# Routing and scattering the last batch earlier in a fused attention and mixture-of-experts kernel

## The chip, the cores and the metric

The kernel runs on one core of one Trainium2 chip. The metric is the device time of one launch in microseconds (us). Engines are named as the profile names them: PE is TensorE (PEld its weight loads), DVE VectorE, ACT ScalarE, POOL GpSimd, and SP the queue that issues most of the direct transfers.

## The reference, cut to what matters

Four batches of 1024 tokens with 128 channels go through one attention layer without learned projections, and then through a layer of eight experts, of which each token takes two. All is float32.

```
x = x + attention(layernorm(x))                  # scores = (x*w_lhs) @ (x*w_rhs).T, softmax, @ x
xf = layernorm(x)                                # 4096 tokens, 128 channels
logits = xf @ router_w.T                         # 8 experts
topk_probs, topk_idx = top_k(softmax(logits), 2) # renormalised to a sum of 1
h = gelu_new(xf @ w_fc[e] + b_fc[e])             # hidden size 512
out = h @ w_proj[e] + b_proj[e]
x = x + sum over the token's two experts of out * gate
```

## The kernel before, in words

**Attention.** The loop over `b` takes one batch of 1024 tokens at a time, as eight token tiles of 128 in two halves. While PE scores batch b, the engines finish batch b-1: the residual (`add_attention`), the second layernorm (`take_stats2`, `take_moments2` on DVE, `scale_ln2` on POOL, `make_h2` and `high_h2` on ACT, `split_h2` on DVE), and the routing.

**Routing a batch** is a chain over four engines. `picks` (DVE, 13 steps) finds the two experts of each token; `find_gap` (DVE) gives the gap of the two logits, and waits for the layernorm scale of the batch's last half from `scale_ln2` on POOL; `gate_powers` (POOL) makes the gate of it; `rank_round` (PE) counts the earlier tokens of each expert; `keep_ranks` and `find_slots` (DVE) make each token's slot numbers and end in the semaphore `meta_made`. Then `dispatch(b, i)` on POOL scatters one tile of rows from `stage` to `slots` in device memory: 16 scatters for a batch (8 token tiles, 2 experts each).

**Experts.** When attention ends, `slots` holds the tokens sorted by expert, and 47 expert tiles are worked through: 24 of 256 rows, then 23 of 128 rows mixed with the last eight large ones. `ORDER` is the sequence. Each engine has a hand-written `step(k)`:

- SP `load(k)` reads the tile from `slots`, once its start is known. Tiles 0 to 7 need table 1 and batches 0 and 1 scattered, tiles 8 to 15 table 2 and batch 2, and tile 16 table 3 and batch 3.
- PE step k: `turn_slots(k+2)` (transposes, L1285), `up(k)` (L1298 to L1300), `down(k-2)` (L1319). So the transposes of tile 8 stand at the start of step 6 and those of tile 16 at the start of step 14.
- ACT step k: `copy_xT(k+2)`, `gelu(k)`, and in the first steps the layernorm of batch 3.
- DVE step k: pieces of the next table (`make_table`), `keep_rows(k)`, then `add_bias(k-3)` and `gate(k-3)`. `down(k)` on PE waits for `add_bias(k-2)`.
- POOL step k: `give_back(k-4)`, a scatter of 128 results for each half tile, once `up(k)` is done.

**The last batch** has no attention behind it that could hide its routing, so its routing is laid between the first expert tiles, at steps that are written out by hand. Its ranks lie in one half of a PSUM bank of `av_ps` that `down` of odd tiles also writes, so one `down` has to wait for `ranks_kept`, which is what `keep_ranks` signals. In the kernel before, PE counts the ranks at the end of step 4 and `down(3)` in step 5 waits for `ranks_kept`; DVE finds the slots in step 5; POOL scatters the batch in its steps 6 and 7:

```
LAST_SCATTERS = {6: range(0, 8), 7: range(8, SCATTERS)}
```

The tables are made by DVE alone: table 2 in steps 0 to 4 (`second_table`), table 3 in 6 to 9 (`late_table`), table 4 in 10 to 13 (`small_table`).

Of the kernel before, what the change touches and what calls it, by code (L numbers as in the profile page):

```python
# [23 lines left out]
def preln_attention_moe(nc, x, w_lhs, w_rhs, router_wT, w_fc, b_fc, w_proj, b_proj, out):  # L24
# [60 lines left out]
    with ExitStack() as ctx:  # L85
# [138 lines left out]
        place = sb("place", [P, H], F32)  # L224
        small_place = sb("small_place", [P, 1], F32)
# [454 lines left out]
        def _(pool):  # L680
# [104 lines left out]

            def gate_powers(r):

                mine = within(r)
                pool.wait_ge(gap_made, r + 1)
                if r >= 1:  # L790
                    pool.wait_ge(slots_made, 4 * r)
                pool.tensor_tensor(gate2[:, mine], euler[:, mine], gap[:, mine], ALU.pow).then_inc(gate_exp, 1)
# [80 lines left out]
            for i in range(11, 15):  # L873
                dispatch(B - 2, i)
            gate_powers(len(ROUNDS) - 1)
            for i in range(15, SCATTERS):
                dispatch(B - 2, i)


            LAST_SCATTERS = {6: range(0, 8), 7: range(8, SCATTERS)}  # L880
# [21 lines left out]
        def _(act):  # L902
# [132 lines left out]
            def step(k, a):  # L1035
                if tile_there(k + 2):
                    copy_xT(k + 2, (a + 2) % NB)
                if tile_there(k):
                    gelu(k, a)

                if k < 2:
                    make_h2(2 * B - 2, 2 + k)
                    if k == 1:
                        high_h2(2 * B - 2)
                if 2 <= k < 6:
                    make_h2(2 * B - 1, k - 2)
                    if k == 5:
                        high_h2(2 * B - 1)
# [9 lines left out]
        def _(pe):  # L1058
# [244 lines left out]
            def down(k, a):  # L1303
# [6 lines left out]
                if k == 3:  # L1310
                    pe.wait_ge(ranks_kept, len(ROUNDS))
# [11 lines left out]
            def step(k, a):  # L1323
# [6 lines left out]
                if k == 4:  # L1330

                    pe.wait_ge(biased_made, 2)
                    rank_round(len(ROUNDS) - 1)
# [18 lines left out]
        def _(dve):  # L1352
# [394 lines left out]
            choose = picks(last)  # L1747

# [38 lines left out]
            def step(k, a):  # L1787

                if k == 0:
                    take_stats2(2 * B - 1)  # L1790
                    take_moments2(2 * B - 1)
                if 1 <= k < 4:
                    steps(choose, (5, 5, 3)[k - 1])
                if k == 3:
                    find_gap(last)
                    split_h2(2 * B - 2)
                if k < 5:
                    steps(second_table, (3, 4, 4, 2, 20)[k])
                if k == 5:
                    keep_ranks(last)  # L1800
                    find_slots(last)
                if k == 7:
                    split_h2(2 * B - 1)
# [57 lines left out]
```

## Time and profile before

| | |
|---|---|
| median of 3 runs | 310.88 us (310.45 to 312.26) |
| span of the profiled execution | 352.5 us |
| time of the profiled execution outside its span | none is shown |
| mean granted clock of TensorE | 0.928 |
| busy in the span | PE 281.2, DVE 230.5, ACT 197.3, POOL 178.5 us |
| scatters to `slots` (POOL) | 64 |
| scatters to `results` (POOL) | 71 |

The profile is of one execution, and its span is 41.6 us longer than the median of the plain runs. A line of a timeline gives the start in us from the span's start, the duration, the engine, the source line, the operation, the output and inputs by the program's names, and in brackets how long the engine had been idle and what ended that. "issue" is idle time in which the profile shows nothing that the engine waited for.

### The profile page before, as it was taken

The page shows a single profiled execution, that of the slowest core. Times are in us where ns is not written, and L with a number is a line of the kernel's source. Part 1 is how long each engine was busy: PE and PEld are TensorE (multiplying, and loading weights), DVE is VectorE, ACT ScalarE, POOL GpSimd, SP SyncE. Part 2 cuts the span into 40 slices and gives each one's busy share as a digit, 9 for nine tenths or more (in the row PEclk, how much of TensorE's full clock was granted, in tenths as well). Part 3 has the DMA queues.
Part 4 walks back from the last instruction along what each step waited for, and adds up shares of the span by engine and source line. Part 5 has one row for each costly group of instructions (what it writes and reads, how often), then busy time and mean ns, then how long its engine had stood idle before and what let it go on. Part 6 is the DMA issues. An engine that isn't in the chain of part 4 may idle for free.

```text
span 352.5 us, 8201 instructions
## 1 busy us (share of the span) xinstructions
PE 281.2 (80%) x2223; PEld 247.1 (70%) x2223; DVE 230.5 (65%) x972; ACT 197.3 (56%) x427; POOL 178.5 (51%) x243
## 2 busy tenths in 40 slices
PE   7999999999949987799496353999969999978200
PEld 3689997989748975689486233999959989977200
DVE  4898988889636896887775224685545555634265
ACT  3363778873648634365694213577658888855100
POOL 8030260285757358585777575455554555444500
PEclk9999999999979999999999685899999999989855
DMA  6930000012110001014213221113222222210199
GB/s 214 420 145 0 3 0 3 0 38 87 55 40 32 2 23 48 31 48 126 68 48 108 70 71 53 47 40 94 74 73 80 70 62 79 65 37 32 37 376 338
DMA packets 15450, 28.51 MB, mean 81 GB/s; under 512 B 3904, under 2 KB 9920, under 8 KB 15152
## 3 DMA queue, kind: packets, MB, share of 16 engines
q1 hardware_dynamic: 10800, 17.93, 15.4%
q0 software_dynamic: 4608, 10.07, 8.6%
q8 instruction: 20, 0.33, 0.4%
q14 instruction: 22, 0.18, 0.2%
HBM read 15.83 MB, written 12.16 MB: 79 GB/s over the span
## 4 chain that ended last, share of the span: by engine, by line
PE 65%; DVE 12%; issue 10%; another core or an unknown queue 4%; ACT 3%; POOL 2%; DMA 2%; POOLq 0%; ACTq 0%; DVEq 0%; SPq 0%
PE av_ps L1319 19%; PE av_ps L1114 14%; PE sc_ps L1300 5%; PE sc_ps L1298 5%; PE sc_ps L1299 4%; DVE neg_piece L1435 4%; PE bank L1285 3%; PE sc_ps L1103 2%; DVE res L1823 2%; PE bank L1090 1%; PE bank L1099 1%; DVE res L1821 1%; PE bank L1092 1%; PE bank L1091 1%
## 5 line engine op out<-in xcount | busy, mean ns | idle before, releaser
L887 POOL DMA_INDIRECT results<-prob,result_row x71 | 68.2, 961 | 62.3 <-PE sc_ps L1300 26.6
L1319 PE MATMUL av_ps<-raw_proj,raw_fc 128*128 x568 | 78.1, 287 | 19.1 <-issue 16.0
L1319 PEld LDWEIGHTS av_ps<-raw_proj,raw_fc 128*128 128x128 f32 x568 | 70.9, 199 | 22.1 <-issue 21.7
L1031 ACT ACTIVATE raw_fc<-sc_ps,bfc,scale_down 128x256 f32<-128x256 f32 (+1 forms) x188 | 80.7, 516 | 3.7 <-remote 3.5
L783 POOL DMA_INDIRECT slots<-stage,slot x64 | 62.6, 978 | 30.4 <-issue 20.2
L1114 PE MATMUL av_ps<-h_all,prob 128*128 128x137 f32 x512 | 74.3, 288 | 0.1
L1114 PEld LDWEIGHTS av_ps<-h_all,prob 128*128 128x128 f32 x512 | 67.7, 192 | 4.2 <-DVE res L1463 1.4
L1777 DVE TENSOR_TENSOR h_all<-av_ps,bpr 128x256 f32<-128x256 f32 (+1 forms) x47 | 16.9, 360 | 63.5 <-remote 35.0
L1023 ACT ACTIVATE h_all<-bank 128x512 f16<-128x512 f16 (+1 forms) x47 | 23.0, 493 | 58.9 <-remote 36.1
L1298 PE MATMUL sc_ps<-h_all,wfc_hi 128*128 128x256 f16 (+1 forms) x188 | 44.2, 252 | 4.2 <-issue 2.9
L1300 PE MATMUL sc_ps<-h_all,wfc_lo 128*128 128x256 f16 (+1 forms) x188 | 44.1, 252 | 2.8 <-issue 2.8
L1299 PE MATMUL sc_ps<-h_all,wfc_hi 128*128 128x256 f16 (+1 forms) x188 | 44.3, 252 | 0.5 <-issue 0.5
L1435 DVE TENSOR_REDUCE neg_piece<-bank 128x1 f32<-128x512 f32 x32 | 22.0, 688 | 14.3 <-remote 6.4
L936 ACT ACTIVATE prob<-sc_ps 128x512 f32<-128x512 f32 x32 | 18.1, 599 | 11.5 <-PE sc_ps L1103 10.3
L1435 DVE TENSOR_REDUCE neg_piece<-sc_ps 128x1 f32<-128x512 f32 x32 | 21.9, 685 | 2.6 <-remote 1.4
L1298 PEld LDWEIGHTS sc_ps<-h_all,wfc_hi 128*128 x188 | 18.8, 100 | 6.8 <-issue 5.1
L926 ACT ACTIVATE again<-bank 128x512 f32<-128x512 f32 x16 | 9.6, 597 | 22.0 <-DVE neg_piece L1435 21.7
L1784 DVE TENSOR_SCALAR prob<-h_all,row_gate 128x128 f32<-128x128 f32 x71 | 20.0, 352 | 1.8 <-DVE h_all L1777 0.2
L1299 PEld LDWEIGHTS sc_ps<-h_all,wfc_hi 128*128 x188 | 18.8, 100 | 3.0 <-issue 2.0
L1300 PEld LDWEIGHTS sc_ps<-h_all,wfc_lo 128*128 x188 | 18.7, 100 | 2.6 <-issue 1.2
L1285 PE MATMUL bank<-ident,slots_in 128*128 128x128 f16 x142 | 16.1, 224 | 4.9 <-issue 4.9
L1090 PE MATMUL bank<-hT_hi,q_hi 128*128 128x512 f32 x32 | 14.6, 457 | 3.7 <-DVE next_slot L1570 2.1
(184 smaller groups left out, 516.7 us busy)
## 6 DMA issues: line engine op xcount, KB each, us to landing
slots_in<-slots SPq DMA_DIRECT2D x24, 132.0 KB
raw_fc<-in_w_fc_dram SPq DMA_DIRECT2D x1, 2048.0 KB, 11.3
raw_proj<-in_w_proj_dram SPq DMA_DIRECT2D x1, 2048.0 KB, 15.7
raw_fc<-results SPq DMA_DIRECT2D x4, 512.0 KB, 5.1
raw_proj<-results SPq DMA_DIRECT2D x4, 512.0 KB, 8.0
out_dram<-res SPq DMA_DIRECT2D x8, 256.0 KB, 6.1
res<-in_x_dram SPq DMA_DIRECT2D x3, 512.0 KB, 5.9
slots_in<-slots SPq DMA_DIRECT2D x23, 66.0 KB
```

The source lines that it names most:

```text
L783: pool.indirect_dma_start(out=slots[:, :], out_offset=bass.IndirectOffsetOnAxis(ap=slot[:, n, k:k + 1], axis=0), in_=stage[:, b % 2, t, :] ...
L887: pool.indirect_dma_start(out=results[:, :], out_offset=bass.IndirectOffsetOnAxis(ap=result_row[a][:, h:h + 1], axis=0), in_=gated[a][h], ...
L1023: act.activation(xT[:, a % NH, 0:n], bank[a % 2][:, :].bitcast(F16)[:, 0:n], ACT.Copy).then_inc(xT_made, 1)
L1031: ins = act.activation(hid[:, a % NH, c, 0:halves_of(k) * P], up_ps(k, c), ACT.Gelu_apprx_tanh, bias=bfc[:, e, c:c + 1], scale=scale_down[ ...
L1114: mm = pe.matmul(att[:, t, 0:AUG], probT[:, m % RING, t * P:(t + 1) * P], h_aug[:, b % 2, exp_rows(n), :], start=(n % BT == 0 and t % 2 == ...
L1285: mm = pe.transpose(o[:, part * w + h * P:part * w + (h + 1) * P], x, ident16[:, :])
L1298: pe.matmul(o, wfc_hi[:, e, of], xT[:, a % NH, 0:w], start=True, stop=False, skip_group_check=True)
L1299: pe.matmul(o, wfc_hi[:, e, of], xT[:, a % NH, w:2 * w], start=False, stop=False, skip_group_check=True)
L1300: mm = pe.matmul(o, wfc_lo[:, e, of], xT[:, a % NH, 0:w], start=False, stop=True, skip_group_check=True)
L1319: mm = pe.matmul(o, hid[:, a % NH, c, rows], wpr[:, e, c, :], start=(c == 0 and h == 0), stop=(c == HC - 1), skip_group_check=True)
L1435: dve.tensor_reduce(neg_piece[:, r // TU, r % TU, c:c + 1], block_bank(n), AX_X, ALU.max, negate=True).then_inc(max_made, 1)
L1784: ins = dve.tensor_scalar(gated[k % NR][h], biased[:, a % NH, h, :], row_gate[:, a, h:h + 1], None, ALU.mult)
```

## The change

Six edits in one. (1) On POOL a memset of one column of a new scratch tile `apart` follows each of the 64 scatters to `slots`; nothing reads it. (2) On POOL `gate_powers` of the last batch stands ahead of the last five scatters of batch 2, not ahead of the last one. (3) The scatters of batch 3 stand in POOL's steps 4 and 6, not 6 and 7. (4) On ACT the layernorm of batch 3 is done in steps 0, 2 and 3, not 0 to 5. (5) On PE the ranks are counted at the end of step 2, not 4, and `down(1)` waits for `ranks_kept`, not `down(3)`. (6) On DVE the statistics, the picks and the gap of the last batch stand ahead of step 0; `keep_ranks` moves from step 5 to 3, `find_slots` from 5 to 4, the two `split_h2` from 3 and 7 to 2 and 5.

```diff
             def dispatch(b, i):
...
                                         in_=stage[:, b % 2, t, :], in_offset=None).then_inc(dispatched[b % 2], 16)
 
+                pool.memset(apart[:, b * K * BT + i:b * K * BT + i + 1], 0.0)
...
             scale_ln2(2 * B - 1)
-            for i in range(11, 15):
+            gate_powers(len(ROUNDS) - 1)
+            for i in range(11, SCATTERS):
                 dispatch(B - 2, i)
-            gate_powers(len(ROUNDS) - 1)
-            for i in range(15, SCATTERS):
-                dispatch(B - 2, i)
...
-            LAST_SCATTERS = {6: range(0, 8), 7: range(8, SCATTERS)}
+            LAST_SCATTERS = {4: range(0, 8), 6: range(8, SCATTERS)}
...
-                if k < 2:
-                    make_h2(2 * B - 2, 2 + k)
-                    if k == 1:
-                        high_h2(2 * B - 2)
-                if 2 <= k < 6:
-                    make_h2(2 * B - 1, k - 2)
-                    if k == 5:
+                if k == 0:
+                    make_h2(2 * B - 2, 2)
+                    make_h2(2 * B - 2, 3)
+                    high_h2(2 * B - 2)
+                if 2 <= k < 4:
+                    make_h2(2 * B - 1, 2 * k - 4)
+                    make_h2(2 * B - 1, 2 * k - 3)
+                    if k == 3:
                         high_h2(2 * B - 1)
...
-                if k == 3:
+                if k == 1:
                     pe.wait_ge(ranks_kept, len(ROUNDS))
...
-                if k == 4:
-
-                    pe.wait_ge(biased_made, 2)
+                if k == 2:
+
                     rank_round(len(ROUNDS) - 1)
...
             choose = picks(last)
+            take_stats2(2 * B - 1)
+            take_moments2(2 * B - 1)
+            steps(choose, 13)
+            find_gap(last)
...
-                if k == 0:
-                    take_stats2(2 * B - 1)
-                    take_moments2(2 * B - 1)
-                if 1 <= k < 4:
-                    steps(choose, (5, 5, 3)[k - 1])
+                if k == 2:
+                    split_h2(2 * B - 2)
                 if k == 3:
-                    find_gap(last)
-                    split_h2(2 * B - 2)
+                    keep_ranks(last)
+                if k == 4:
+                    find_slots(last)
                 if k < 5:
                     steps(second_table, (3, 4, 4, 2, 20)[k])
                 if k == 5:
-                    keep_ranks(last)
-                    find_slots(last)
-                if k == 7:
                     split_h2(2 * B - 1)
```

**DVE, where step 0 begins.** Before, behind the variance of the batch's last half, three steps of table 2 and then `keep_rows(0)`, which waits for tile 0:

```order
L1491 TENSOR_SCALAR var<-moments 128x4 [waits ln2_rstd,ln2_moments]
L485 TENSOR_TENSOR per_expert<-per_expert,ends 128x8 [waits dve_chain]
L488 TENSOR_TENSOR past<-tile_id,per_expert 128x64 [waits dve_chain]
L492 TENSOR_SCALAR capped<-per_expert 128x16 [waits dve_chain]
L1762 SCALAR_TENSOR_TENSOR gate_parts<-slots_in,of_expert 128x2 [waits xs_in0]
L1764 SCALAR_TENSOR_TENSOR gate_parts<-slots_in,of_expert 128x2
L1766 SCALAR_TENSOR_TENSOR chosen_row<-slots_in,of_expert 128x2
L1769 TENSOR_TENSOR row_gate<-gate_parts 128x2 [waits row_parts]
```

Of the change, from the end of the picks (`taken`) to the same place, with the step that waits for `ln2_rstd` (POOL's scale) and the load of the expert numbers ahead of them:

```order
L1542 TENSOR_TENSOR pick<-pick,first_id 128x64 [waits route_chain]
L1550 TENSOR_TENSOR taken<-pick 128x2x32 [waits route_chain]
L1556 TENSOR_TENSOR step_down<-best 128x8
L1561 TENSOR_TENSOR gap<-step_down,rstd 128x8 [waits gate_exp,ln2_rstd,route_chain]
L587 TENSOR_LOAD turn_experts
L587 ISA x2
L487 TENSOR_TENSOR per_expert<-per_expert,ends 128x8 [waits dve_chain]
L490 TENSOR_TENSOR past<-tile_id,per_expert 128x64 [waits dve_chain]
L494 TENSOR_SCALAR capped<-per_expert 128x16 [waits dve_chain]
L1768 SCALAR_TENSOR_TENSOR gate_parts<-slots_in,of_expert 128x2 [waits xs_in0]
L1770 SCALAR_TENSOR_TENSOR gate_parts<-slots_in,of_expert 128x2
```

All 13 picks, the gap and its wait now stand ahead of the table and of tile 0's rows.

**PE, the ranks.** Before, the count (L1136, L1142) stands behind `down(2)` and ahead of the transposes of tile 7 (`xs_in7`):

```order
L1319 MATMUL av_ps<-raw_proj,raw_fc 128x128 x5
L1136 MATMUL av_ps<-taken,before 128x80 [waits taken_made,biased_made]
L1142 MATMUL av_ps<-taken,ones 128x72
L1142 MATMUL av_ps<-taken,ones 128x64
L1142 MATMUL av_ps<-taken,ones 128x56
L1142 MATMUL av_ps<-taken,ones 128x48
L1142 MATMUL av_ps<-taken,ones 128x32
L1142 MATMUL av_ps<-taken,ones 128x24
L1142 MATMUL av_ps<-taken,ones 128x16
L1142 MATMUL av_ps<-taken,ones 128x8
L1285 MATMUL bank<-ident,slots_in 128x128 [waits xT_made,xs_in7]
L1285 MATMUL bank<-ident,slots_in 128x128 x3
```

Of the change it stands behind `down(0)`, ahead of the transposes of tile 5 (the line numbers are three higher), and no longer waits for `biased_made`:

```order
L1322 MATMUL av_ps<-raw_proj,raw_fc 128x128 x5
L1139 MATMUL av_ps<-taken,before 128x80 [waits taken_made]
L1145 MATMUL av_ps<-taken,ones 128x72
L1145 MATMUL av_ps<-taken,ones 128x64
L1145 MATMUL av_ps<-taken,ones 128x56
L1145 MATMUL av_ps<-taken,ones 128x48
L1145 MATMUL av_ps<-taken,ones 128x32
L1145 MATMUL av_ps<-taken,ones 128x24
L1145 MATMUL av_ps<-taken,ones 128x16
L1145 MATMUL av_ps<-taken,ones 128x8
L1288 MATMUL bank<-ident,slots_in 128x128 [waits xT_made,xs_in5]
L1288 MATMUL bank<-ident,slots_in 128x128 x3
```

The count has moved two tiles forward, past two `up` and two `down`.

**POOL, behind the scale of the last half.** Before, four scatters to `slots`, the gate, one scatter, and then the results of tiles 0 and 1:

```order
L748 TENSOR_TENSOR shift<-neg_mean,rstd 128x4 [waits ln2_mean,ln2_rstd]
L783 DMA slots<-stage,slot 32768x132 [waits meta_made,h2lo_made] x4
L792 TENSOR_TENSOR gate<-euler,gap 128x8 [waits slots_made,gap_made]
L783 DMA slots<-stage,slot 32768x132 [waits meta_made,h2lo_made]
L887 DMA results<-prob,result_row 22528x128 [waits gated_made,row_made,stepped]
L887 DMA results<-prob,result_row 22528x128
L887 DMA results<-prob,result_row 22528x128 [waits gated_made,row_made,stepped]
L887 DMA results<-prob,result_row 22528x128
```

Of the change the gate stands first; each scatter has a memset behind it:

```order
L750 TENSOR_TENSOR shift<-neg_mean,rstd 128x4 [waits ln2_mean,ln2_rstd]
L796 TENSOR_TENSOR gate<-euler,gap 128x8 [waits slots_made,gap_made]
L785 DMA slots<-stage,slot 32768x132 [waits meta_made,h2lo_made]
L788 MEMSET apart 128x1
L785 DMA slots<-stage,slot 32768x132 [waits meta_made,h2lo_made]
L788 MEMSET apart 128x1
L785 DMA slots<-stage,slot 32768x132 [waits meta_made,h2lo_made]
L788 MEMSET apart 128x1
```

The eight first scatters of the last batch (not shown) follow directly on the 16th of batch 2, ahead of the results of tile 0, where before the results of tiles 0 and 1 stood ahead of them.

## Rows read from the trace of the kernel before

**Rows 1.** The page: span, busy time of each engine, shares of the chain.

```profile
span 352.5 us, 8201 instructions
...
PE 281.2 (80%) x2223; PEld 247.1 (70%) x2223; DVE 230.5 (65%) x972; ACT 197.3 (56%) x427; POOL 178.5 (51%) x243
...
PE 65%; DVE 12%; issue 10%; another core or an unknown queue 4%; ACT 3%; POOL 2%; DMA 2%; POOLq 0%; ACTq 0%; DVEq 0%; SPq 0%
```

**Rows 2.** Windows: busy us of each engine, TensorE clock, in one stretch.

```profile
core 0: us, PE busy (x) PEld busy (x) DVE busy (x) ACT busy (x) POOL busy (x), PEclk, DMA share, GB/s
...
192.00:195.00 3.00, 0.27 (x1) 0.37 (x2) 0.00 (x0) 0.00 (x0) 2.26 (x3) 1.00 0.31 99
```

**Rows 3.** Timeline of PE: start, us, instruction, at three tiles, and its end.

```profile
187.74 0.39 PE L1285 MATMUL bank<-ident,slots_in 128*128 128x128 f16 x4
...
225.46 0.39 PE L1285 MATMUL bank<-ident,slots_in 128*128 128x128 f16 x4
...
238.74 0.39 PE L1285 MATMUL bank<-ident,slots_in 128*128 128x128 f16 x4
...
327.55 1.15 PE L1319 MATMUL av_ps<-raw_proj,raw_fc 128*128 x8 [0.24 <-ACT raw_fc L1031]
```

**Rows 4.** Windows over a fall of the clock.

```profile
97.10:100.50 3.40, 1.37 (x10) 1.08 (x8) 0.00 (x0) 0.00 (x0) 2.54 (x3) 1.00 0.15 51
100.50:107.30 6.80, 4.21 (x14) 3.73 (x15) 3.38 (x15) 5.09 (x11) 3.45 (x5) 0.50 0.07 22
```

**Rows 5.** Timeline of DVE: last batch and the tiles' own work.

```profile
168.00 0.87 DVE L1478 BATCH_NORM_STATS2 stats<-res 128x6 f32<-128x128 f32 x4 [0.75 <-issue]
...
173.23 0.16 DVE L496 TENSOR_TENSOR per_expert<-per_expert,used 128x8 f32<-128x8 f32 x1
...
174.19 0.21 DVE L1762 SCALAR_TENSOR_TENSOR gate_parts<-slots_in,of_expert 128x2 f32<-128x2 f32 x1
...
174.85 0.22 DVE L1544 SCALAR_TENSOR_TENSOR lg<-pick,lg 128x64 f32<-128x64 f32 x1
...
178.20 0.68 DVE L1498 TENSOR_TENSOR stage<-h,stage 128x512 f16<-128x512 f32 x1
```

**Rows 6.** Timeline of DVE: ranks and slots of the last batch.

```profile
185.24 0.23 DVE L1567 TENSOR_TENSOR rank<-av_ps,next_slot 128x64 f32<-128x64 f32 x1 [1.32 <-PE av_ps L1142]
...
185.58 0.35 DVE L1577 TENSOR_TENSOR pick<-pick,rank 128x64 f32<-128x64 f32 x2
...
187.45 0.22 DVE L1762 SCALAR_TENSOR_TENSOR gate_parts<-slots_in,of_expert 128x2 f32<-128x2 f32 x1
```

**Rows 7.** Timeline of POOL: scatters before the last batch.

```profile
172.10 1.05 POOL L745 TENSOR_TENSOR rstd<-var,minus_half 128x4 f32<-128x4 f32 x1
...
177.88 0.95 POOL L783 DMA_INDIRECT slots<-stage,slot  x1 [0.30 <-issue]
178.86 1.67 POOL L792 TENSOR_TENSOR gate<-euler,gap 128x8 f32<-128x8 f32 x1
180.73 1.03 POOL L783 DMA_INDIRECT slots<-stage,slot  x1 [0.20 <-issue]
182.06 0.96 POOL L887 DMA_INDIRECT results<-prob,result_row  x1 [0.30 <-issue]
...
185.80 0.95 POOL L887 DMA_INDIRECT results<-prob,result_row  x1 [1.52 <-PE sc_ps L1300]
```

**Rows 8.** Groups of POOL: the scatter and a memset of one column.

```profile
L783 POOL DMA_INDIRECT slots<-stage,slot x64 | 62.6, 978 | 30.4 <-issue 20.2 <-DVE stage L1595 7.3 <-ACT prob L936 2.8
...
L701 POOL MEMSET digit<- 128x1 f32 x8 | 0.3, 99 | 0.0
```

**Rows 9.** Timeline of SP: the issue of tile 8's load.

```profile
185.04 0.00 SPq L662 DMA_DIRECT2D slots_in<-slots  x1
```

**Rows 10.** Timeline of PE: the projection of tile 1.

```profile
177.52 1.95 PE L1319 MATMUL av_ps<-raw_proj,raw_fc 128*128 x16
```

**Rows 11.** Timeline of ACT: its start of tile 1.

```profile
173.33 0.60 ACT L1023 ACTIVATE h_all<-bank 128x512 f16<-128x512 f16 x1 [3.26 <-remote]
```

More of the change, by code:

```diff
@@ L224, in preln_attention_moe @@
         place = sb("place", [P, H], F32)
+        apart = sb("apart", [P, K * NT], F32)
         small_place = sb("small_place", [P, 1], F32)
```

## The prediction

> **What bounds the kernel now.** I read the page first: the chain that ended last lies 65% on PE, 12% on DVE and 10%, some 35 us, on "issue", time in which nothing that the profile shows was waited for [rows 1]. So PE sets the end, and a tenth of the span has no cause in the program. A window of 3 us at 192 shows what such time looks like: PE is busy 0.27 us, DVE and ACT not at all, while POOL goes on scattering [rows 2]; one at 97 to 100 us is of the kind too [rows 4]. The timeline of PE gives its size. From the transposes of tile 12 (step 10, 225.46) to those of tile 16 (step 14, 238.74) a step lasts 3.32 us; from tile 8's (step 6, 187.74) to tile 12's four steps last 37.72 us, 24.4 more than 4 x 3.32 [rows 3]. With this and the smaller ones of its kind (about 4 us at 98 to 102, 2 us of half clock behind it [rows 4], 3 us of ACT at 170 to 173 [rows 11], and by the same windows some 9 us elsewhere) I come to about 42 us. The span is 352.5 us [rows 1] and no time outside it is shown; the plain runs take 310.88. So I hold that the plain runs don't have these stretches (352.5 - 42 = 310.5), take them out, and give what is left in the clock of the profile, around the edit. The sum below is a difference of two such reckonings, added to 310.88.
>
> **The place that counts.** Two loads on SP are held by scatters: tile 8's by batch 2, tile 16's by batch 3. If PE comes to step 14 before tile 16 is there, the last batch's scatters bound the kernel; if it comes later, PE's own steps do. I need four times: when PE comes to step 14 and when tile 16 lies in SBUF, each before and after.
>
> **Before, tile 16.** POOL ends batch 2's last scatter at 181.76 and does the results of tile 0 at 182.06. Those of tile 1 begin at 185.80, 1.52 us late, since they wait for `up(5)` [rows 7]; without the 1.4 us that DVE's and PE's gaps cost here, about 184.5. From there POOL isn't idle: 2 results, 8 scatters, 2 results, 8 scatters, 20 in all, each 0.96 us and 0.30 us of issue [rows 7, 8], 1.26 us: the last ends at 184.5 + 25.2 = 209.7. From the end of batch 2's last scatter to the issue of tile 8's load lie 185.04 - 181.76 = 3.3 us [rows 7, 9]. From issue to transposes 187.74 - 185.04 = 2.7 us is the upper bound [rows 3, 9]; PE came there straight from `down(3)`, so I take 1.2. Tile 16 can be turned at 209.7 + 3.3 + 1.2 = 214.2 (213.6 to 216, with 2.7 and POOL's start at 185.8 for the upper end). **Before, PE.** Step 6 begins at 187.74 [rows 3], or about 1.2 us earlier without the gaps: 186.5. Eight steps of 3.32 are 26.6: step 14 at 213.1. So the scatters decide, by about 1 us: 214.2.
>
> **After, the new wait.** PE counts the ranks behind `down(0)`, but `down(1)` waits for `ranks_kept`, and DVE keeps the ranks only in step 3. What DVE has ahead of that: (a) `find_gap` waits for POOL's scale, ready at 172.10 + 1.05 = 173.15 [rows 7]; that lies behind six scatters whose memsets add 0.2, so the gap is made by 173.4. The 11 picks and `taken`, ahead of it, are 0.26 us each and fit between 168.7 and 172.2. (b) Loading the expert numbers, 0.75 (the idle time ahead of the statistics, at the same place of the program) [rows 5]. (c) `keep_rows` three times, 174.85 - 174.19 = 0.66, say 0.7: 2.1 [rows 5]. (d) Table 2: four steps are 174.19 - 173.23 = 0.96, eleven 2.3 [rows 5]. (e) `split_h2` 0.6 (its 0.68 overlaps the next) [rows 5]. (f) The ranks 185.58 - 185.24 = 0.34 [rows 6]. Sum: 173.4 + 0.75 + 2.1 + 2.3 + 0.6 + 0.34 = 179.5. In the profile before, `down(1)` began at 177.52 [rows 10], and that was late: `up(3)` waited for ACT, which had lost 3.26 us [rows 11]; without it about 175.3. PE stands still from 175.3 to 179.5, 4.2 us. Queued behind it are `turn_slots(6)`, `up(4)` and all after; ACT has `gelu(2)` behind it and waits with PE.
>
> From 179.5 PE has `down(1)` (1.8) and steps 4 and 5 (2 x 3.32): step 6 at 188.0. Nothing on DVE holds it longer: `add_bias(0)` ends at 181.0, then the slots (187.45 - 185.58 = 1.87 [rows 6]), the rest of table 2 (7 steps, 1.3), `keep_rows(4)` and `add_bias(1)` come to 185.8, and `down(3)` starts at 186.2. Table 2 is ready at 184.6, batch 2's last scatter ends at 182.1 with the memsets, so tile 8's load is out by 185.7 and doesn't hold PE either. ACT's layernorm of two token tiles a step costs it 0.5 us more in steps 0, 2 and 3, and is covered by PE's wait; without the wait it would delay `gelu(3)` by under 1 us, which PE needs two steps later. Step 14 follows at 188.0 + 26.6 = 214.6.
>
> **The clock.** In 97.1 to 100.5 PE was busy 1.37 of 3.4 us, and in the next 6.8 us its granted clock was 0.50, that is 1.2 GHz [rows 4]. A stand of 4.2 us is of that kind. PE's work from 179.5 on would then run at half speed for 2 to 4 us and lose 1 to 2 us. The trace can't say that it falls; I put it at 60%. Step 14 is at 214.6 without and 215.6 to 216.6 with it.
>
> **After, tile 16.** `meta_made` comes with the slots, at 183.3. POOL waits for it from 182.1: here the earlier place of the scatters buys an idle engine. Then 8 scatters, 4 results, 8 scatters. **The memset** measures 0.10 us [rows 8]. Between two scatters lie 0.30 us; around the gate they are 0.03 and 0.20 [rows 7], so a memset between should make it 0.03 + 0.10 + 0.20 = 0.33, 0.03 more; at most it adds its whole 0.10. I take 0.03 (the gate is the nearest row) and 1.29 a scatter: 183.5 + 16 x 1.29 + 4 x 1.26 = 209.2, with 0.10 a memset 210.3. Tile 16 can be turned at 209.2 + 3.3 + 1.2 = 213.7 (to 216.3). For the other 48 memsets, 1.4 to 4.8 us of POOL, the cover is POOL's waits for DVE and ACT between the batches (10.1 us ahead of scatters alone, 7.3 + 2.8 [rows 8]). One rule speaks against the price: the Trainium skill (SBUF — State Buffer, section "SBUF: two separate sides") says that GpSimd and a VectorE operation of certain kinds lock each other out of a shared port for a whole instruction. By it each of the 16 could wait for a DVE operation, 0.2 to 0.7 us, and tile 16 would come up to 11 us later. The scatters of this trace don't show it: they take 0.95 and 0.96 us beside a busy DVE and 0.96 in the mean [rows 7, 8].
>
> **The sum.** Before, tile 16 is turned at 214.2 (scatters). After, it is 214.6 without a fall of the clock and about 216.1 with it (PE). The difference is +0.4 or +1.9, weighed +1.3; so 312.2 us. Behind step 14 nothing changes: PE ended 90 us later (327.55 + 1.15 - 238.74 [rows 3]), 83 without some 7 us of empty stretches, at 297; POOL's 65 remaining results, 82 us from 209.7 on, are done at 292.
>
> **The rivals.** (A) *The wait at `down(1)` costs nothing*, since tile 16 comes later than I reckon in both kernels (the upper ends, 216 before). Then the time is the difference of the two scatter chains, 213.7 - 214.2 = -0.5, or 0 with dearer memsets: 310.4 to 311. For it: no trace shows tile 16 late, since in the profile PE was later than all scatters. (B) *Faster*: PE's stand is shorter than 1 us because DVE gets to the ranks by 176, and what goes is the wait for the ranks in step 5 and for tile 16: at most 214.2 - 213.1 = 1.1 us, with 1.3 for a later start of POOL 2.4 us: 308.5 to 309.3. It decides if DVE's 6.1 us between gap and ranks are 3 or less. Or the empty stretches aren't gone in the plain runs and the memsets, which set the scatters apart, shorten them: 305 to 309. For it, they all lie where scatters follow one another; against it, the 42 us. (C) *Worse*: POOL's scale comes later, or the clock falls twice, or the memsets meet the port: 314 to 317.
>
> **How the numbers follow.** The forecast case (PE bound, +0.2 to +3) gets 0.52, A 0.20, B 0.15, C 0.13. The measurement tells apart about 0.5%, 1.55 us. Of the forecast case about half lies above +1.55; with C, slower gets 0.39. B gives faster 0.15; A and the other half are 0.46. The range goes from inside B to inside C: 309.3 to 315.3.
>
> **What would show it.** In the profile after: PE idle ahead of the first matmul of `down(1)`, released by DVE's `next_slot`, 3 to 5 us; the clock at 0.50 behind it; `find_gap` on DVE released by POOL's `rstd`; POOL idle about 1.3 us ahead of the first scatter of batch 3; a memset of 0.10 us and scatters 1.29 us apart. I am wrong if `down(1)` starts without a wait, if tile 16's transposes wait for SP in the kernel after, or if the span falls to near the plain time, which would say that the memsets act on the empty stretches.
>
> The Trainium skill (Runtime: NRT & Kernel Launch, section "The ~15µs preamble/postamble breakdown") says that a profile's total lies some 6 us above the plain time whatever the kernel; here it is 41.6, so by that rule 35 us would be real, the end would hang on the empty stretches, and case B's second half would gain weight. That no number above rests on.

## The result, and the profile after

| | kernel before | changed kernel |
|---|---|---|
| median of plain runs | 310.81 us (310.2 to 312.52, 12 runs) | 312.82 us (311.84 to 314.54, 12 runs) |
| ratio to before | | 1.0067, 95% interval 1.0049 to 1.0085 |
| profiled execution, span | 352.5 us [rows 1] | 311.0 us, own time 312.78 us |

The change costs 2.0 us, 0.7%. 312.2 was predicted, in a range of 309.3 to 315.3. The page of the changed kernel, its span, engine and chain lines:

```profile
span 311.0 us, 8265 instructions
...
PE 269.4 (87%) x2223; PEld 241.8 (78%) x2223; DVE 230.1 (74%) x972; ACT 196.7 (63%) x427; POOL 185.5 (60%) x307
...
PE 60%; POOL 12%; issue 10%; DVE 8%; DMA 4%; ACT 3%; SPq 1%; POOLq 1%; DVEq 0%; ACTq 0%
```

The span is 41.5 us shorter than that of [rows 1], though the kernel got slower. The empty stretches of [rows 2] are gone. So no time of this page may be set against one of [rows 1 to 11] without a common mark. I use `rstd` on POOL, the scale that the gap needs: it starts at 172.10 before [rows 7] and at 164.04 here, so 8.06 us less. The timeline of PE, from the projection of tile 1 to the transposes of tiles 6, 8 and 16:

```profile
171.78 3.78 PE L1322 MATMUL av_ps<-raw_proj,raw_fc 128*128 x16 [6.30 <-DVE next_slot L1572]
175.35 0.63 PE L1288 MATMUL bank<-ident,slots_in 128*128 128x128 f16 x4
...
182.60 0.39 PE L1288 MATMUL bank<-ident,slots_in 128*128 128x128 f16 x4
...
209.16 0.39 PE L1288 MATMUL bank<-ident,slots_in 128*128 128x128 f16 x4
```

PE stands still for 6.30 us, for the ranks, as forecast. The 16 matmuls of `down(1)` then take 3.78 us instead of the 1.95 of [rows 10]. Tile 16 is there when PE wants it: its row has no idle time. The timeline of DVE shows why the ranks are late:

```profile
165.18 0.20 DVE L1561 TENSOR_TENSOR gap<-step_down,rstd 128x8 f32<-128x8 f32 x1 [1.86 <-issue]
166.12 0.17 DVE L487 TENSOR_TENSOR per_expert<-per_expert,ends 128x8 f32<-128x8 f32 x1 [0.74 <-issue]
...
171.38 0.16 DVE L1572 TENSOR_TENSOR next_slot<-next_slot,av_ps 128x8 f32<-128x8 f32 x1
...
172.48 0.42 DVE L1783 TENSOR_TENSOR h_all<-av_ps,bpr 128x256 f32<-128x256 f32 x1
```

DVE is idle for 1.86 us ahead of `find_gap`. The row calls it "issue", but POOL's `rstd` below ends at 165.09, 0.09 us before the gap starts, and the gap waits for it. Then the expert numbers are loaded (the 0.74 us of idle time in the second row), and steps 0 to 2 follow. The last row is `add_bias(0)`. The windows (stretches of 5 us, columns as in [rows 2]) show the clock:

```profile
165.00:170.00 5.00, 0.48 (x5) 0.19 (x2) 3.81 (x21) 1.05 (x3) 4.27 (x8) 0.98 0.04 14
170.00:175.00 5.00, 3.22 (x15) 3.23 (x16) 4.59 (x29) 4.38 (x10) 3.16 (x6) 0.50 0.16 54
175.00:180.00 5.00, 5.00 (x44) 4.56 (x44) 3.81 (x22) 2.30 (x5) 3.47 (x7) 0.84 0.27 64
```

PE's granted clock is 0.50 (1.2 GHz) behind the stand. POOL's timeline, the scale and the gate, the end of batch 2, the start and the end of batch 3:

```profile
164.04 1.05 POOL L747 TENSOR_TENSOR rstd<-var,minus_half 128x4 f32<-128x4 f32 x1
...
165.46 1.64 POOL L796 TENSOR_TENSOR gate<-euler,gap 128x8 f32<-128x8 f32 x1
...
173.42 0.12 POOL L788 MEMSET apart<- 128x1 f32 x1
175.96 0.96 POOL L785 DMA_INDIRECT slots<-stage,slot  x1 [2.41 <-DVE stage L1597]
176.91 0.11 POOL L788 MEMSET apart<- 128x1 f32 x1
177.22 0.96 POOL L785 DMA_INDIRECT slots<-stage,slot  x1 [0.19 <-issue]
...
199.96 0.95 POOL L785 DMA_INDIRECT slots<-stage,slot  x1 [0.19 <-issue]
```

Scatters start 1.26 us apart, which is also what 0.96 us and 0.30 us of idle time make without a memset [rows 7, 8]. The memset lies in what had been 0.30 us of idle time, of which 0.19 are left.

### The profile page after: what moved, and what is told of

It is laid out like the page before. It is cut to its first block, busy times and chain, and to the rows that moved or that the text cites. A ratio compares the mean times of both kernels' runs of the same rounds, so it can differ in the third digit from the quotient of the medians.

```text
span 311.0 us, 8265 instructions
## 1 busy us (share of the span) xinstructions
PE 269.4 (87%) x2223; PEld 241.8 (78%) x2223; DVE 230.1 (74%) x972; ACT 196.7 (63%) x427; POOL 185.5 (60%) x307
## 4 chain that ended last, share of the span: by engine, by line
PE 60%; POOL 12%; issue 10%; DVE 8%; DMA 4%; ACT 3%; SPq 1%; POOLq 1%; DVEq 0%; ACTq 0%
PE av_ps L1322 21%; PE av_ps L1117 10%; POOL slots L785 8%; PE sc_ps L1301 5%; PE sc_ps L1302 4%; PE sc_ps L1303 4%; DVE neg_piece L1437 4%; DMA raw_proj<-results 3%; PE bank L1288 2%; PE bank L1093 1%; PE sc_ps L1106 1%; PE bank L1095 1%; PE bank L1094 1%; POOL apart L788 1%; SPq L675 1%
## 5 line engine op out<-in xcount | busy, mean ns | idle before, releaser
L1322 PE MATMUL av_ps<-raw_proj,raw_fc 128*128 x568 | 74.2, 282 | 6.4 <-DVE next_slot L1572 6.3
L1322 PEld LDWEIGHTS av_ps<-raw_proj,raw_fc 128*128 128x128 f32 x568 | 68.7, 196 | 7.4 <-issue 7.0
L1117 PE MATMUL av_ps<-h_all,prob 128*128 128x137 f32 x512 | 73.2, 285 | 0.7 <-DVE lg_part L1468 0.6
L1117 PEld LDWEIGHTS av_ps<-h_all,prob 128*128 128x128 f32 x512 | 66.8, 190 | 4.6 <-DVE res L1465 1.7
L1301 PE MATMUL sc_ps<-h_all,wfc_hi 128*128 128x256 f16 (+1 forms) x188 | 43.0, 248 | 1.1 <-ACT raw_fc L1033 1.1
L1302 PE MATMUL sc_ps<-h_all,wfc_hi 128*128 128x256 f16 (+1 forms) x188 | 42.9, 247 | 0.0
L1303 PE MATMUL sc_ps<-h_all,wfc_lo 128*128 128x256 f16 (+1 forms) x188 | 42.9, 247 | 0.0
L948 ACT ACTIVATE h<-res,shift,rstd 128x128 f32<-128x128 f32 x32 | 14.2, 486 | 6.9 <-DVE stage L1500 4.0
```

What stands on the lines that cost most here:

```text
L1117: mm = pe.matmul(att[:, t, 0:AUG], probT[:, m % RING, t * P:(t + 1) * P], h_aug[:, b % 2, exp_rows(n), :], start=(n % BT == 0 and t % 2 == ...
L1301: pe.matmul(o, wfc_hi[:, e, of], xT[:, a % NH, 0:w], start=True, stop=False, skip_group_check=True)
L1302: pe.matmul(o, wfc_hi[:, e, of], xT[:, a % NH, w:2 * w], start=False, stop=False, skip_group_check=True)
L1303: mm = pe.matmul(o, wfc_lo[:, e, of], xT[:, a % NH, 0:w], start=False, stop=True, skip_group_check=True)
L1322: mm = pe.matmul(o, hid[:, a % NH, c, rows], wpr[:, e, c, :], start=(c == 0 and h == 0), stop=(c == HC - 1), skip_group_check=True)
```

## The experiments

The kernel before was timed in each group of runs: 310.41, 310.38 and 310.37 us. Ratios are to these; a ratio can differ from the quotient of two medians by 0.1%. The theories of an expectation are numbered in it.

**1. The memsets alone, on the kernel before.**

```diff
                 pool.indirect_dma_start(out=slots[:, :], ...).then_inc(dispatched[b % 2], 16)
+                pool.memset(apart[:, b * K * BT + i:b * K * BT + i + 1], 0.0)
```

> The kernel before with one thing of the change alone: GpSimd clears a column of the scratch tile behind each scatter to the slots. Theory 1 (the memsets lie in time in which GpSimd would be idle between two scatters anyway, and nobody's work waits for them): time as of before, 310.8 us within 0.5%; and since the empty stretches of before's profile (rows 2, about 42 us) are a distortion of the profiled execution, they go with the memset alone: span about 309 instead of 352.5, and its rows then show for the first time how the plain run of before goes. Theory 2 (each memset delays the next scatter by its 0.1 us, 128 times, and the queue behind POOL ends later): 1 us or more slower. Theory 3 (the empty stretches are also in plain runs, in part): faster by more than 1 us.

Measured: 310.59 us, ratio 1.0013 (0.9996 to 1.0031); span 310.7 us. The time is that of theory 1, and theories 2 and 3 fall. The empty stretches are gone too, as theory 1 said; whether the memsets took them away, only experiment 2 can tell.

**2. The changed kernel without the memsets.**

```diff
-                pool.memset(apart[:, b * K * BT + i:b * K * BT + i + 1], 0.0)
```

> The changed kernel without the memsets. Theory 1 (the memset acts on the profile alone): time as of the changed kernel, 312.8 us (+0.6% to before), but the profiled span back at about 350 us with empty stretches where GpSimd scatters back to back. Theory 2 (the memsets are what the 2 us went to): back at 310.8 us. Theory 3 (the memsets hid a part of the loss): 314 us or more.

Measured: 312.75 us, ratio 1.0084 (1.0061 to 1.0108), as the changed kernel; span 309.8 us. The timeline of POOL there:

```profile
198.70 0.96 POOL L784 DMA_INDIRECT slots<-stage,slot  x1 [0.30 <-issue]
199.96 1.01 POOL L784 DMA_INDIRECT slots<-stage,slot  x1 [0.30 <-issue]
```

The memsets cost and give nothing. The second half of theory 1, in both experiments, is wrong: the empty stretches are away without the memset too, and experiments 5, 6 and 7 are further kernels without it, with spans of 308.5 to 310.8 us. Only the one profile of the kernel before has them. One of 35 plain runs of it, timed beside experiments 6 to 9, took 470.83 us. No profile of such a run was taken, so that this has to do with the empty stretches isn't shown.

**3. The ranks first.** `down(1)` should no longer wait for them.

```diff
             find_gap(last)
+            keep_ranks(last)
...
-                if k == 3:
-                    keep_ranks(last)
```

> The changed kernel, but VectorE takes the ranks off the PSUM bank right behind find_gap, ahead of its step 0, instead of ahead of step 3. Theory 1 (the stand of 6.30 us ahead of down(1) is what the change costs): next_slot is made about 166.5 instead of 171.4, the stand ahead of down(1) shrinks to about 1 us and TensorE's clock does not fall; but tile 8 is then wanted at about 177 and SyncE issues its load at 177.3 and it lands about 2 us later, so about 2 us of the 5 come back as a stand ahead of turn(8). Net 2 to 4 us faster than the changed kernel: 309 to 311 us. Theory 2 (the returns of the rows on GpSimd or the tail set the end, the stand is covered): 312.8 us, no change.

Measured: 310.2 us, ratio 0.9985 (0.9962 to 1.0008). The size is as forecast, the place isn't. PE's timeline, `down(1)` and `down(2)`:

```profile
167.43 2.05 PE L1322 MATMUL av_ps<-raw_proj,raw_fc 128*128 x16 [0.51 <-ACT raw_fc L1033]
...
174.54 3.10 PE L1322 MATMUL av_ps<-raw_proj,raw_fc 128*128 x16 [3.53 <-DVE h_all L1784]
```

The stand isn't ahead of tile 8 but ahead of `down(2)`, for `add_bias(0)`. Two things count for what follows. The loss is gone although DVE still stands idle for `rstd` ahead of its step 0 (1.89 us) and `add_bias(0)` is as late as in the changed kernel. And tile 16 is there in time:

```profile
201.41 0.96 POOL L785 DMA_INDIRECT slots<-stage,slot  x1 [0.19 <-issue]
```

```profile
207.94 0.39 PE L1288 MATMUL bank<-ident,slots_in 128*128 128x128 f16 x4
```

All times of this one execution are 1.5 us late (`rstd` starts at 165.51, not 164.04); the last section says why.

**4. The ranks back at their old place**, all else as changed.

```diff
-                if k == 1:
+                if k == 3:
                     pe.wait_ge(ranks_kept, len(ROUNDS))
...
-                if k == 2:
+                if k == 4:
+                    pe.wait_ge(biased_made, 2)
                     rank_round(len(ROUNDS) - 1)
...
-                if k == 3:
-                    keep_ranks(last)
-                if k == 4:
-                    find_slots(last)
+                if k == 5:
+                    keep_ranks(last)
+                    find_slots(last)
```

> The changed kernel with one thing put back: the last rank round at the end of TensorE's step 4 (behind the wait for biased_made 2), the wait for ranks_kept ahead of down(3), ranks and slots on VectorE in step 5. Picks, gap, layer norm and GpSimd's scatters (from step 4 on) stay as changed. Theory 1 (the wait at down(1) is the loss): no stand at down(1), the first scatter of batch 3 about 3 us later than changed, which is still in time for tile 16 (its load went out at 203.0, TensorE wants it at about 209): time 2 us or more under the changed kernel, 309 to 311 us. Theory 2 (something else of the change costs, as the picks made ahead of step 0 or the three make_h2 in the first steps of ScalarE): still about 312.8 us.

Measured: 313.13 us, ratio 1.009 (1.0073 to 1.0107), so the loss stays. PE's timeline at `down(2)` and tile 16, and POOL's first and last scatter of batch 3:

```profile
172.65 2.88 PE L1322 MATMUL av_ps<-raw_proj,raw_fc 128*128 x16 [3.97 <-DVE h_all L1784]
...
208.44 0.40 PE L1288 MATMUL bank<-ident,slots_in 128*128 128x128 f16 x4 [1.97 <-DMA slots_in<-slots]
```

```profile
178.84 0.96 POOL L785 DMA_INDIRECT slots<-stage,slot  x1 [5.47 <-DVE stage L1501]
...
203.02 0.96 POOL L785 DMA_INDIRECT slots<-stage,slot  x1 [0.19 <-issue]
```

Without the wait at `down(1)` PE stands 3.97 us at `down(2)`. Even so it is ready for tile 16 at 208.44 - 1.97 = 206.47, 2.7 us sooner than in the changed kernel (209.16). But the edit also put the slots back to step 5. The first scatter comes 2.9 us later, as expected, and that isn't "still in time": PE waits 1.97 us for tile 16. So the number is that of theory 2, but the run doesn't speak against theory 1: what PE won, the scatters took. Experiment 3, which left the slots where the change has them, kept it. The next four try the change's parts one by one.

**5. ScalarE's part alone, on the kernel before**: three or two pieces of layer norm in one step.

```diff
-                if k < 2:
-                    make_h2(2 * B - 2, 2 + k)
...
+                if k == 0:
+                    make_h2(2 * B - 2, 2)
+                    make_h2(2 * B - 2, 3)
+                    high_h2(2 * B - 2)
+                if 2 <= k < 4:
+                    make_h2(2 * B - 1, 2 * k - 4)
+                    make_h2(2 * B - 1, 2 * k - 3)
```

> The kernel before with ScalarE's part alone: the third and fourth normalised tile of a half batch and high_h2 bundled into step 0, and two each into steps 2 and 3. Theory 1 (ScalarE has the time, VectorE alone makes the loss): 310.4 us within 0.5%. Theory 2 (the two extra activations ahead of copy_xT(3) and gelu(1) hold TensorE in its first steps): 311 us or more, with a stand ahead of up(1) or down(0).

Measured: 310.29 us, ratio 1.0002 (0.9986 to 1.0018). ScalarE's part costs nothing. Since its time is that of the kernel before, its profile serves from here on for the kernel before without empty stretches: span 308.5 us, and `rstd` ends within 0.2 us of the changed kernel's. PE's timeline (`down(2)`, tile 8, tile 16) and DVE's (`find_gap`, `add_bias(0)`), each by itself:

```profile
170.77 3.58 PE L1320 MATMUL av_ps<-raw_proj,raw_fc 128*128 x16 [2.19 <-DVE h_all L1778]
...
177.97 0.40 PE L1286 MATMUL bank<-ident,slots_in 128*128 128x128 f16 x4
...
206.34 0.40 PE L1286 MATMUL bank<-ident,slots_in 128*128 128x128 f16 x4 [1.40 <-DMA slots_in<-slots]
```

```profile
168.34 0.17 DVE L1560 TENSOR_TENSOR gap<-step_down,rstd 128x8 f32<-128x8 f32 x1
...
170.10 0.42 DVE L1778 TENSOR_TENSOR h_all<-av_ps,bpr 128x256 f32<-128x256 f32 x1
```

Here is what the profile of before couldn't show: PE already stood 2.19 us for `add_bias(0)`, `down(2)` behind it takes 3.58 us (granted clock 0.66 from 170 to 175 us), and PE waits 1.40 us for tile 16. So the scatters bound the kernel before, and they hide the stand and the clock. Experiment 1's execution (the same with memsets) agrees: there the clock stayed at 1.00 behind a stand of 2.23 us, `down(2)` took 2.05 us, and PE still waited 1.29 us for tile 16. POOL's last scatter here:

```profile
200.62 0.96 POOL L783 DMA_INDIRECT slots<-stage,slot  x1 [0.31 <-issue]
```

`find_gap` has no wait, since it comes 3.4 us after `rstd`'s end.

**6. VectorE's part alone, on the kernel before.**

```diff
             choose = picks(last)
+            take_stats2(2 * B - 1)
+            take_moments2(2 * B - 1)
+            steps(choose, 13)
+            find_gap(last)
...
-                if k == 0:
-                    take_stats2(2 * B - 1)
-                    take_moments2(2 * B - 1)
-                if 1 <= k < 4:
-                    steps(choose, (5, 5, 3)[k - 1])
                 if k == 3:
-                    find_gap(last)
                     split_h2(2 * B - 2)
```

> The kernel before with VectorE's part alone: the last statistics, the 13 picks and find_gap stand ahead of step 0; ranks, slots, GpSimd's and ScalarE's order stay as before. Theory 1 (VectorE reaches add_bias(0) 2.3 us later since it stands idle for GpSimd's rstd2 ahead of step 0): the stand ahead of down(2) grows from 2.23 to 4 us or more, time 312 to 313.2 us. Theory 2 (the loss lies in ScalarE's bundled make_h2, or in the gates on GpSimd ahead of scatters 11 to 14): 310.4 us, as before.

Measured: 312.1 us, ratio 1.0046 (1.0018 to 1.0074). DVE's, PE's and POOL's timelines (POOL: first result of tile 1, last scatter):

```profile
165.12 0.20 DVE L1559 TENSOR_TENSOR gap<-step_down,rstd 128x8 f32<-128x8 f32 x1 [1.84 <-issue]
...
172.14 0.42 DVE L1781 TENSOR_TENSOR h_all<-av_ps,bpr 128x256 f32<-128x256 f32 x1
```

```profile
172.81 3.77 PE L1319 MATMUL av_ps<-raw_proj,raw_fc 128*128 x16 [4.46 <-DVE h_all L1781]
...
208.69 0.40 PE L1285 MATMUL bank<-ident,slots_in 128*128 128x128 f16 x4 [1.20 <-DMA slots_in<-slots]
```

```profile
179.43 0.96 POOL L887 DMA_INDIRECT results<-prob,result_row  x1 [2.92 <-PE sc_ps L1300]
...
203.48 0.96 POOL L783 DMA_INDIRECT slots<-stage,slot  x1 [0.30 <-issue]
```

`add_bias(0)` comes 2.04 us later than in experiment 5 (172.14 - 170.10), and PE's stand grows from 2.19 to 4.46. The loss, 1.4 us by the ratio and 1.7 by the medians, then comes by way of the scatters, though the edit doesn't touch them: `up(5)` stands behind `down(2)`, POOL waits 2.92 us for it with the results of tile 1, its last scatter starts 2.9 us later than in experiment 5, and PE waits 1.20 us for tile 16.

**7. The scatters' steps alone, on the kernel before.**

```diff
-            LAST_SCATTERS = {6: range(0, 8), 7: range(8, SCATTERS)}
+            LAST_SCATTERS = {4: range(0, 8), 6: range(8, SCATTERS)}
```

> The kernel before with LAST_SCATTERS {4: 0 to 7, 6: 8 to 15} alone. Theory 1 (GpSimd is the queue that sets tile 16: in the trace of the kernel before with the memset 22 indirect transfers run from 175.6 to 203.3, 1.265 us apart; the new order has two fewer of them ahead of the last scatter, but starts only when the slots are there at 177.7, 2 us later): the last scatter ends when it did, the stand ahead of turn(16) stays about 1.3 us, and the time is 310.4 us within 0.5%. Theory 2 (the order alone brings tile 16 sooner): stand gone, 309 us. Theory 3 (the rows of tiles 0 and 1 given back later hold VectorE's gate up): 311.5 us or more.

Measured: 310.96 us, ratio 1.001 (0.9974 to 1.0046). No gain: POOL's last scatter starts at 201.95 and PE waits 2.22 us for tile 16, not less than the 1.40 of experiment 5.

**8. The gap moved out of DVE's way**, in the changed kernel.

```diff
             steps(choose, 13)
-            find_gap(last)
...
                 if tile_there(k):
                     keep_rows(k, a)
+                if k == 0:
+                    find_gap(last)
```

> The changed kernel with find_gap (VectorE's wait for GpSimd's rstd2, 1.86 us idle in the trace of the changed kernel) moved from ahead of step 0 to the end of step 0, where rstd2 is there. New theory 1 after the run with the ranks put back, which kept the loss with the stand moved to down(2): the loss is that VectorE comes to the end of its step 3 about 2.3 us later than before, and 1.9 of that is this idle time. Then next_slot and add_bias(0) come 1.7 to 1.9 us sooner, the stand ahead of down(1) goes from 6.30 to about 4.5 us, and the time is about 311 us (1.5 to 2 under the changed kernel's 312.8). Theory 2 (the idle time only stands in for the next wait of VectorE; TensorE's clock and the stand are as before): 312.8 us.

Measured: 310.05 us, ratio 0.9984 (0.9956 to 1.0013), 2.8 us under the changed kernel: the whole loss and more than the 1.5 to 2 us expected, by moving one instruction behind step 0. DVE's timeline (`find_gap`, ranks, `add_bias(0)`) and PE's:

```profile
165.47 0.17 DVE L1561 TENSOR_TENSOR gap<-step_down,rstd 128x8 f32<-128x8 f32 x1
...
169.50 0.16 DVE L1572 TENSOR_TENSOR next_slot<-next_slot,av_ps 128x8 f32<-128x8 f32 x1
...
170.60 0.42 DVE L1782 TENSOR_TENSOR h_all<-av_ps,bpr 128x256 f32<-128x256 f32 x1
```

```profile
169.90 3.67 PE L1322 MATMUL av_ps<-raw_proj,raw_fc 128*128 x16 [4.33 <-DVE next_slot L1572]
```

The gap is made at nearly the same time as in the changed kernel (165.47 against 165.18), but DVE has done step 0 in the meantime, and the ranks come 1.88 us sooner. Tile 8 is turned at 180.05, 2.55 us sooner than in the changed kernel: the 0.7 us beyond the 1.88 go with the clock, which is back at 1.00 from 175 to 180 us (there 0.84).

**9. Gap and ranks at the end of step 0.** The same, and `keep_ranks(last)` behind `find_gap(last)`, taken out of step 3.

```diff
                 if k == 0:
                     find_gap(last)
+                    keep_ranks(last)
...
-                if k == 3:
-                    keep_ranks(last)
```

> The same with the ranks taken off the bank right behind find_gap, at the end of step 0. Theory 1: no stand at down(1), the stand ahead of down(2) goes from 3.53 us (in the run with the ranks first) to about 1.6 us; tile 16 is there in time as in that run: about 308.5 to 309.5 us, faster than the kernel before by 0.3 to 0.6%. Theory 2 (another transfer, tile 8 or tile 16, takes up what the stand gives back): 310.2 us, as with the ranks first.

Measured: 308.85 us (308.5 to 310.4), ratio 0.9939 (0.9912 to 0.9966), faster than both kernels. All that is left of the stands from 165 us on, in PE's timeline:

```profile
166.09 2.05 PE L1322 MATMUL av_ps<-raw_proj,raw_fc 128*128 x16 [0.62 <-DVE next_slot L1572]
...
171.16 2.05 PE L1322 MATMUL av_ps<-raw_proj,raw_fc 128*128 x16 [1.49 <-DVE h_all L1782]
...
175.73 2.05 PE L1322 MATMUL av_ps<-raw_proj,raw_fc 128*128 x16 [0.99 <-DVE h_all L1782]
...
178.44 0.40 PE L1288 MATMUL bank<-ident,slots_in 128*128 128x128 f16 x4 [0.67 <-DMA slots_in<-slots]
```

Its windows from 165 to 180 us grant 1.00: four short stands, and each `down` behind a stand takes 2.05 us, not over 3.

**10. More of the same**, on experiment 9: `add_bias` and `gate` first in DVE's steps 3 and 4, the first `split_h2` in step 3 instead of 2, `find_slots` behind the rest of table 2; **11.** the same with

```diff
-            LAST_SCATTERS = {4: range(0, 8), 6: range(8, SCATTERS)}
+            LAST_SCATTERS = {4: range(0, 8), 5: range(8, SCATTERS)}
```

> The version with gap and ranks at the end of step 0, and VectorE does add_bias and gate of tiles 0 and 1 first in its steps 3 and 4, then split_h2 of the seventh half batch, and in step 4 find_slots behind the rest of table 2. The remaining stands of that version are 1.49 and 0.99 us ahead of down(2) and down(3), 0.67 ahead of turn(8). Theory 1 (VectorE's lateness is all that holds TensorE until tile 8): add_bias(0) about 1.7 us sooner, both stands gone; tile 8 then comes about as before, so that about 2 us come back ahead of turn(8), which table 2, made 0.5 to 1 us sooner, cuts a little: 308 to 308.8 us. Theory 2 (GpSimd's row of indirect transfers is the bound behind it: in that version it runs without idle time from 173 to past 205, and the slots come about 1.5 us later now): the time moves to a stand ahead of turn(16), 309 to 309.5 us, no better or worse than 308.85.

> The same with LAST_SCATTERS {4: 0 to 7, 5: 8 to 15}, so that the two results transfers of tile 1 follow the last scatter. Theory 1 (TensorE waits for tile 16 behind GpSimd's last scatter): the last scatter ends 2.5 us sooner and the time is 0.5 to 1 us under the run beside it. Theory 2 (nothing waits at tile 16): the same time as the run beside it within 0.3 us, or later, if VectorE waits for the rows given back.

Measured: 310.36 us, ratio 1.0002 (0.999 to 1.0015), and 309.05 us, ratio 0.9966 (0.9947 to 0.9985). PE's timeline at tile 16 in the one and the other:

```profile
206.57 0.40 PE L1288 MATMUL bank<-ident,slots_in 128*128 128x128 f16 x4 [1.23 <-DMA slots_in<-slots]
```

```profile
205.39 0.39 PE L1288 MATMUL bank<-ident,slots_in 128*128 128x128 f16 x4
```

In the first the bias stands are gone, but PE waits 1.74 us in `up(5)` for ACT instead and comes to tile 8 no sooner (178.61, in experiment 9 178.44). The slots are made later, POOL's last scatter starts at 200.52 instead of experiment 9's 198.49, and PE waits 1.23 us for tile 16: theory 2's mechanism, and dearer than it said (310.36 against 309 to 309.5). In the second two results less stand ahead of the last scatter (198.02), the wait is gone and with it 1.3 us. So the scatters are the other bound, about a microsecond away. Experiment 9 stays the fastest.

## Why the prediction was right, and where not

Times of the profile of before are given minus 8.06 us where they are compared. Two chains meet at tile 16, as the prediction has it: PE's own steps, and the scatters that its load waits for. The table has both, from the profiled executions. PE is ready where its idle time at tile 16 starts; the last column is the time of that same execution, not the median.

| kernel | PE ready for tile 16 | last scatter starts | tile 16 turned | time |
|---|---|---|---|---|
| before, ScalarE's part (5) | 204.9 | 200.6 | 206.3, scatters | 310.3 |
| before, VectorE's part (6) | 207.5 | 203.5 | 208.7, scatters | 312.6 |
| changed | 209.2 | 200.0 | 209.2, PE | 312.8 |
| changed, ranks and slots back (4) | 206.5 | 203.0 | 208.4, scatters | 312.4 |
| changed, gap behind step 0 (8) | 206.6 | 198.3 | 206.6, PE | 310.7 |
| changed, gap and ranks behind step 0 (9) | 205.2 | 198.5 | 205.2, PE | 309.2 |

In all six the time is 103.6 to 104.1 us more than the moment at which tile 16 is turned. So the differences arise before it.

**Held.** That the plain runs lack the empty stretches. That the scatters bound the kernel before and PE the changed one. Tile 16 turned by the scatters in the kernel before at 214.2 - 8.1 = 206.1: 206.34 in experiment 5. PE ready for it at 213.1 - 8.1 = 205.0: 206.34 - 1.40 = 204.9. The wait at `down(1)` with DVE's sum from the gap to the ranks, 6.1 us: 171.54 - 165.38 = 6.2. `add_bias(0)` done at 181.0 - 8.1 = 172.9: 172.48 + 0.42. The last scatter's end in the changed kernel, 209.2 - 8.1 = 201.1: 200.91. No stand at tile 16. In experiment 5 tile 16 is turned at 206.34, in the changed kernel at 209.16: +2.8 us, where +1.9 was given for a fall of the clock. The medians say +2.0.

**Mis-sized: "PE stands still from 175.3 to 179.5, 4.2 us".** It was 6.30. The end was right (179.5 - 8.1 = 171.4), in part by luck: term (d), eleven steps at the 0.24 us that its row gives, is 2.6 and not 2.3. PE came sooner, at 165.5 instead of 167.2. The sum took 2.2 us off the 177.52 of [rows 10], where ACT alone had lost 3.26 [rows 11].

**Mis-sized: the loss to the clock, "1 to 2 us".** From `down(1)` to tile 8 the sum gave 1.8 + 2 x 3.32 = 8.4 us at full speed; the trace has 182.60 - 171.78 = 10.8, so 2.4 us. The sum for the kernel before left out its own stand of 2.19 us and the clock behind it, and still came out right at step 14 (205.0 against 204.9). The 1.2 us that it took off for gaps was a guess, so that is in part luck.

**Mis-sized: the memset and POOL's idle time.** 0.00 us a memset instead of 0.03 (1.26 us from scatter to scatter), and 2.41 us ahead of batch 3's first scatter instead of 1.3: it starts at 175.96, not at 183.5 - 8.1 = 175.4. Sixteen times 0.03 is the same half microsecond, so two errors cancel in the last scatter's end. The longer waits for the shared port, by the Trainium skill (SBUF — State Buffer, section "SBUF: two separate sides"), are in no scatter of the changed kernel between 167 and 202 us: they take 0.95 to 1.08 us beside DVE's work.

**The step "the new wait": right, but not the whole.** Experiment 3 takes the wait at `down(1)` away and the loss is gone, with DVE's idle time still there and `add_bias(0)` as late as in the changed kernel (173.87 less the 1.47 us by which that execution is late is 172.40, against 172.48). Experiment 8 leaves the wait and makes the ranks 1.88 us sooner, and the loss is gone as well. So the changed kernel loses by both together: PE asks for the ranks two tiles sooner, and DVE, which stands idle for `rstd` ahead of step 0, makes them too late for that. The prediction has both, as its waits in (a) and at `down(1)`. What it lacks is that DVE's idle time costs by itself, too: on the kernel before it makes 1.4 to 1.7 us by way of `up(5)`, the results of tile 1 and the last scatter (experiment 6). In experiment 4 PE wins 2.7 us and the scatters come 3.1 us later. Its median lies 1 us above experiment 6's (313.13 and 312.1), while the two profiled executions, at 312.41 and 312.63, don't differ that way; this stays open.

**The rivals.** A (hidden by tile 16) was true in part: PE reaches tile 8 4.6 us later than in experiment 5 and tile 16 only 2.8 later; of the other 1.8 us, 1.4 had been lost to the wait for tile 16 anyway. B's second half and its sign that the memsets act on the empty stretches are refuted by experiments 1 and 2. The shorter span, which I had named as a proof of it, came of one odd profile. C didn't come. The rule of the Trainium skill (Runtime: NRT & Kernel Launch, section "The ~15µs preamble/postamble breakdown"), by which 35 us of the 41.6 would have been real, was rightly given no weight: all twelve further profiles have spans 1.7 to 1.9 us below the time of the same execution, and lie near the medians.

## What to carry to other kernels

An instruction moved ahead in an in-order queue moves the wait in front of it, too: ask when its operand is ready, and put it behind work that needs nothing new. If a wait taken away doesn't bring its time back, look at where the two chains meet before the idea is dropped: experiment 4 brought PE 2.7 us sooner and by the same edit the scatters 3.1 us later. One late engine can show up in several places; here it was `down(1)`, `down(2)`, `down(3)` or tile 16, whichever was asked first. And before a profile much longer than the plain runs is reasoned on, a second profile, of a variant that changes nothing, is worth more than any subtraction.

## What the runs showed that I hadn't expected

One execution's profile had about 42 us of empty stretches which none of the twelve other profiles has, with or without memsets. A memset of 0.11 us between two indirect transfers on POOL was free here: both ways they start 1.26 us apart.

TensorE's clock can fall early and cost as much as the change. In experiments 1 and 3 the profiled run has 11 matmuls less in this window than the changed kernel's (x132, clock 1.00):

```profile
20.00:40.00 20.00, 20.00 (x121) 17.48 (x122) 16.63 (x57) 10.40 (x21) 3.20 (x7) 0.91 0.02 7
```

This row is of experiment 1. Its own time is 312.49 us beside a median of 310.59, that of experiment 3 311.48 beside 310.2. `rstd` on POOL starts 1.8 us later than in experiment 5 in the one, and 1.5 us later than in the changed kernel in the other, so that time is lost long before the experts. PE was not idle in that window in either case. In the 5 us before it PE was busy 4.53 us in both, as in the changed kernel (4.54), where the clock stayed at 1.00. What makes it fall in some executions wasn't tried. Behind PE's stand in step 4 it varies as well: 2.19 us in experiment 5 and the clock falls, 2.23 us in experiment 1 and it doesn't.
